# Matmuls of 512 columns issued as two of 256, one half of a PSUM bank after the other

## The reference, cut to what matters

```
nf, df = scan forward of (exp(k)*v, exp(k));  nb, db = the same backward
base = sigmoid(r) * ((nf + nb - ekv + euk*v) / max(df + db - ek + euk, 1e-8))
h = einsum('bsd,fd->bsf', base * (0.8 + 0.2*tf), W1)     # 1024 -> 4096
a = gelu(clip(round(h / 0.1)) * 0.1)
x + einsum('bsf,df->bsd', a, W2)                         # 4096 -> 1024
```

## Time and profile before

| | |
|---|---|
| time, median of 2 runs | 1900.47 us (1900.39 to 1900.55) |
| span of the profiled execution, first to last instruction | 1898.6 us |
| what lies around it, against the median | 1.9 us |
| TensorE busy | 1788.5 us (94%) |
| weight loads busy | 805.5 us (42%) |
| VectorE busy | 1342.6 us (71%) |
| ScalarE busy | 735.2 us (39%) |

### The profile page before, as it was taken

How to read it: one execution, slowest core, us unless ns; L and a number is a source line. 1 busy time by engine, 2 the same in 40 slices (tenths; PEclk the granted TensorE clock), 3 DMA queues, 4 the chain that set the end, 5 groups by cost and what they waited for, 6 DMA issues and landing times.

```text
span 1898.6 us, 24557 instructions
## 1 busy us (share of the span) xinstructions
PE 1788.5 (94%) x8194; PEld 805.5 (42%) x8194; DVE 1342.6 (71%) x1916; ACT 735.2 (39%) x1200; POOL 8.1 (0%) x20
## 2 busy tenths in 40 slices
PE   1358999999999999999999999999999999999998
PEld 0123444444444444444444444444444444444443
DVE  8986896698966796599986786588985777622111
ACT  4446611465116621366214641176313652034200
POOL 0000000000000000000000000000000000000000
PEclk9678999999999999999999999999999999999999
DMA  8585444434453344434443334534354334433133
GB/s 236 140 191 175 144 166 139 166 118 154 160 173 131 124 147 158 169 116 155 166 157 142 120 139 144 180 130 147 145 177 154 107 142 155 160 112 122 67 123 104
DMA packets 79576, 277.80 MB, mean 146 GB/s; under 512 B 9264, under 2 KB 9264, under 8 KB 62640
## 3 DMA queue, kind: packets, MB, share of 16 engines
q1 hardware_dynamic: 78768, 260.61, 39.3%
q0 software_dynamic: 768, 16.78, 4.3%
HBM read 277.36 MB, written 33.55 MB: 164 GB/s over the span
## 4 chain that ended last, share of the span: by engine, by line
PE 91%; DVE 5%; issue 2%; DMA 1%; ACT 0%; DVEq 0%; SPq 0%
PE h_ps L393 47%; PE h_ps L378 45%; DMA V<-in_fside_dram 1%; DVE DEN L636 1%; DVE EKP L633 0%; DVE NUM L660 0%; DVE NUM L681 0%; DVE DEN L664 0%; DVE EKV L630 0%; DVE DEN L670 0%; DVE V L667 0%; DVE EKVP L628 0%; DVE RCP L652 0%; DVE DEN L644 0%; DVE mix L588 0%
## 5 line engine op out<-in xcount | busy, mean ns | idle before, releaser
L393 PE MATMUL h_ps<-act,w_ring 128*128 128x512 f16 x4096 | 885.4, 379 | 0.0
L378 PE MATMUL h_ps<-mix,w_ring 128*128 128x512 f16 x3968 | 860.8, 380 | 8.6 <-ACT q L495 8.6
L393 PEld LDWEIGHTS h_ps<-act,w_ring 128*128 128x128 f16 x4096 | 400.8, 98 | 483.3
L378 PEld LDWEIGHTS h_ps<-mix,w_ring 128*128 128x128 f16 x3968 | 388.9, 98 | 479.2 <-ACT q L495 9.1
L805 DVE SCALAR_TENSOR_TENSOR act<-a,act 128x512 f32 (+1 forms) x256 | 164.9, 686 | 227.5 <-ACT act L508 227.3
L488 ACT ACTIVATE mix<-NUM 128x512 f32 (+1 forms) x64 | 40.1, 626 | 670.5 <-DVE NUM L783 623.9
L495 ACT ACTIVATE q<-h_ps 128x512 int16<-128x512 f32 x256 | 148.1, 591 | 333.2 <-PE h_ps L378 331.8
L812 DVE SCALAR_TENSOR_TENSOR xy<-h_ps,xy 128x512 f32<-128x512 f32 x64 | 43.9, 687 | 222.6 <-PE h_ps L393 222.6
L780 DVE RECIPROCAL DEN<-DEN 128x512 f32<-128x512 f32 x56 | 187.4, 3347 | 0.0
L502 ACT ACTIVATE a<-q 128x512 f32<-128x512 int16 x256 | 146.7, 622 | 0.6
L508 ACT ACTIVATE act<-a 128x512 f32 (+1 forms) x256 | 145.4, 617 | 0.0
(11 more groups left out here) (91 smaller groups left out, 903.7 us busy)
## 6 DMA issues: line engine op xcount, KB each, us to landing
w_ring<-w_half SPq DMA_DIRECT2D x128, 1024.0 KB, 4.9
chk_full<-in_w_dram SPq DMA_DIRECT2D x64, 512.0 KB, 5.7
V<-in_fside_dram SPq DMA_DIRECT2D x64, 256.0 KB, 4.3
R<-in_x_dram SPq DMA_DIRECT2D x64, 256.0 KB, 4.1
w_half<-in_w_dram POOLq DMA_DIRECT2D x16, 1024.0 KB, 11.4
xy<-in_x_dram SPq DMA_DIRECT2D x64, 256.0 KB, 2.7
chk_half<-w_half SPq DMA_DIRECT2D x64, 256.0 KB, 5.9
out_dram<-xy SPq DMA_DIRECT2D x64, 256.0 KB, 5.2
```

Source lines behind the costliest of these rows:

```text
L378: mm = pe.matmul(h_ps[k][j][:, :], weights[:, k, j, c, :], rhs, start=(c == 0 and p == 0), stop=(c == CT - 1 and p == len(parts(c)) - 1))
L393: mm = pe.matmul(y_ps[k][:, :], weights[:, k, f, :], rhs, start=(f == 0 and p == 0), stop=(f == FT - 1 and p == len(parts(f)) - 1))
```

## The change

`hidden` and `output` get a list of halves of the columns. For each tile, all matmuls of columns 0 to 255 are issued first, then all of columns 256 to 511, with the same weights again. The waits stand where they stood, ahead of a tile; in `output` those for `s_alo` are all in the first half. `start` (which empties the bank) is set on the first matmul of the first half alone. `first_hidden` isn't changed, and the general path asks for `WHOLE`, the old form.

```diff
+            HALF = [slice(0, T // 2), slice(T // 2, T)]
+            WHOLE = [slice(0, T)]
...
-            def hidden(n, i, weights, parts, loaded):
+            def hidden(n, i, weights, parts, loaded, halves=HALF):
...
-                        for c in range(CT):
-                            for p, rhs in enumerate(parts(c)):
-                                mm = pe.matmul(h_ps[k][j][:, :], weights[:, k, j, c, :], rhs,
-                                               start=(c == 0 and p == 0),
-                                               stop=(c == CT - 1 and p == len(parts(c)) - 1))
+                        for half in halves:
+                            for c in range(CT):
+                                for p, rhs in enumerate(parts(c)):
+                                    mm = pe.matmul(h_ps[k][j][:, half], weights[:, k, j, c, :], rhs[:, half],
+                                                   start=(half is halves[0] and c == 0 and p == 0),
+                                                   stop=(c == CT - 1 and p == len(parts(c)) - 1),
+                                                   skip_group_check=True)
                         mm.then_inc(s_h, 1)
...
-            def output(n, i, weights, parts, loaded, s_act, start):
+            def output(n, i, weights, parts, loaded, s_act, start, halves=HALF):
...
-                    for f in range(FT):
-                        if k == 0:
-                            pe.wait_ge(s_act[f % FPS], start + STEPS * n + f // FPS + 1)
-                        for p, rhs in enumerate(parts(f)):
-                            mm = pe.matmul(y_ps[k][:, :], weights[:, k, f, :], rhs,
-                                           start=(f == 0 and p == 0),
-                                           stop=(f == FT - 1 and p == len(parts(f)) - 1))
+                    for half in halves:
+                        for f in range(FT):
+                            if k == 0 and half is halves[0]:
+                                pe.wait_ge(s_act[f % FPS], start + STEPS * n + f // FPS + 1)
+                            for p, rhs in enumerate(parts(f)):
+                                mm = pe.matmul(y_ps[k][:, half], weights[:, k, f, :], rhs[:, half],
+                                               start=(half is halves[0] and f == 0 and p == 0),
+                                               stop=(f == FT - 1 and p == len(parts(f)) - 1),
+                                               skip_group_check=True)
                     mm.then_inc(s_y, 1)
```

More of the change, by code:

```diff
@@ L418, in general_block @@
                     hidden(n, i, w1_gen, lambda c: [mix_gen[:, slot, c, :]],
-                           lambda k: pe.wait_ge(s_wgen[k], 16 * (2 * ITER * m + i + 1)))
+                           lambda k: pe.wait_ge(s_wgen[k], 16 * (2 * ITER * m + i + 1)), WHOLE)
                 with pe.Fori(0, ITER) as i:
                     output(n, i, w2_gen, lambda f: [act_gen[:, f, :]],
-                           lambda k: pe.wait_ge(s_wgen[k], 16 * (2 * ITER * m + ITER + i + 1)), s_gelu, 0)
+                           lambda k: pe.wait_ge(s_wgen[k], 16 * (2 * ITER * m + ITER + i + 1)), s_gelu, 0, WHOLE)
             pe.wait_ge(s_flag, 1)
```

## The result

1934.88 us median (1934.33 to 1935.43, 2 runs) against 1900.47: a ratio of 1.018, 95% interval 1.015 to 1.021. The change costs 34 us. The forecast was 1925 us in a range of 1912 to 1950, so the sign and the range held, and the middle was 10 us low; the narrower range that the prediction adds up from its small terms, 1916 to 1934, was missed by 1 us. The interval holds 1.02, so whether the loss is more than the 2% that the prediction takes for a clear change isn't decided. The span of the profiled execution is 1931.1 us against 1898.6, 32.5 us more; the medians differ by 34.4. What lies outside the span is 3.2 and 3.0 us in the two runs of the change; in the other 37 runs of the kernel before it is 2.4 to 3.3, so the 1.9 beside the profile of before was unusually small.

The account below looks back on a forecast made before the run. The prediction took TensorE's unbroken chain of matmuls as the bound. Span 1898.6 + 20.1 (pace) + 4.0 (wait in block 0) = 1922.7 us; with 1.9 between span and median, 1924.6, stated as 1925, range 1912 to 1950.

Parts of the forecast that it names:

- small terms: Half clock after the wait in block 0, 0 to +3 us, and code fetches at outer jumps, 0 to +5 us.
- Term 1: In both products, 8018 matmuls each become two, paying a fixed 2.5 ns twice: 218.4 in place of 215.8 ns, +20.1 us.
- one that goes with columns: Rival, 5%: the 2.5 ns of each matmul go with its column count, so the pace costs nothing extra: 1904.5 us.
- Term 2: In block 0's `output`, TensorE wants activation tile 30 before DVE has written it, and waits: +4.0 us.
- 2.7 us of margin: In block 1's `output`, DVE's last tiles are done 3.9 us after the start, needed at 6.6: no wait.
- Term 3: After TensorE's 3.5 us stop in block 0, the clock might fall to half: taken as 0, range 0 to +3 us.
- Term 4: At two outer jumps, twice as many instructions might force code fetches: 0 to +5 us, taken as 0.
- The rival of the load: Every matmul of both products: the weight load comes into the open; with 16 ns settling, +77 us, 2002 us; 18%.
- 9 ns of margin: In both products, the 98 ns weight load still fits into a half matmul's 106.7 ns; the margin was 115 ns before.
- The faster rival: Half matmuls overlap down to a weight load's 98 ns, 180 us less than forecast: 1745 us; 2%.

Follow-up runs that it names:

- The kernel with the pace alone: The whole change plus TensorE's outer loop written out and, in the second product, both halves of an activation tile issued one behind the other: 1919.68 us, ratio 1.0098.
- its own control: The kernel before with only TensorE's outer loop written out: 1899.64 us against 1900.95 for the kernel before, ratio 0.9994.
- first and second experiment: The change in one product alone, against the kernel before: first product (`hidden`) 1910.53 us, ratio 1.0054; second product (`output`) 1917.48 us, ratio 1.0091.
- the kernel with the tiles side by side: The whole change, but in the second product both halves of an activation tile are issued one behind the other: 1925.02 us, ratio 1.0132 against the kernel before.
- The kernel before with a large body: The kernel before, matmuls still of 512 columns, with two turns written out in each inner body except the first of block 0: 1901.70 us, ratio 1.0004.
- four quarters: The change with both products in four parts of 128 columns in place of two of 256: one run, 1983.16 us.
- the three written-out kernels: TensorE's outer loop written out in the change (1926.72 us), in the kernel before (1899.64), and in the change with each tile's halves adjacent in the second product (1919.68).

## Why the prediction was right, and where it was short

**Term 1, the pace: right.** 111.79 / 1024 = 109.17 ns, the predicted 109.2, and 19.2 us for fifteen products. The choice between a fixed part and one that goes with columns is settled by three widths and a mixed pair: 55.84 - 53.33 = 2.51 ns at 128, 109.17 - 106.67 = 2.50 at 256, 215.84 - 213.33 = 2.51 at 512, and the pair of 320 and 192 costs the same 218.3 ns as two of 256. The kernel with the pace alone is 20.0 us above its own control.

**Term 2, the wait in block 0: right.** 3.63 us, as said, at tile 30, released by DVE L812. The 0.4 for tile 31 can't be read apart: the clock was at half by then, and the two matmuls of tile 30 took up much of it. It is in the second product alone (first and second experiment), and goes when a tile is wanted later (1925.0 us, no such wait). In block 1 and later no such wait shows, as was argued from the 2.7 us of margin.

**Term 3, the clock: taken at 0, was 2.9.** I argued from one wait of 8.6 us, where the clock fell 4.3 us after TensorE stopped, that a stop of 3.5 us would be too short. It wasn't: the clock was at half when TensorE restarted at 243.33, 3.6 us after, and at the second jump after a stop of 2.5 us. Behind the first jump (2.70 us) and behind both of the kernel with the tiles side by side (2.23 and 2.49) it wasn't. The length of the stop alone doesn't decide it: in the kernel with k = 0 kept at 512 the clock fell behind one of 2.19 us and not behind one of 2.24. Nor is the price fixed: with the loop written out, the same wait in block 0 (3.7 us) was followed by half clock from about 243 to 249 us and cost 2.9, the 3 us that I had named and set aside. One row doesn't bound when the clock falls; the spread is to be taken, here 0 to 2.9 us for each stop of some 2 to 4 us. That its two falls came to 2.9 us, inside the 0 to 3 I gave for one, is luck.

**Term 4, the code: taken at 0, was 5.6.** This is the step that failed. The bound (5 us for both jumps) was near, but not the value: I let matmuls already issued cover the fetch, without asking how long they last. A jump with a fetch takes 3.6 to 3.8 us in the change, and the issued matmuls last 1.8 of it. The kernel before with a large body shows the cover at 216 ns each, with 0.4 and 0.5 us left over. The control shows that the loop itself costs nothing. (The upper end of 1934 was also added wrongly: 1924.6 + 3 + 5 is 1932.6.) The Trainium skill's 2048 instructions (Runtime: NRT & Kernel Launch, Instruction fetch mechanics) gave the right answer for the change, 2,101, by my count above it; but 1,845 and 1,717 stopped too, and 1,589 didn't, so less than the 2048 can be used for a loop. The two lines of 256 that the same section gives (for a buffer of 32 KiB; TensorE's is 128) are refuted for TensorE again, in inner bodies of 512 instructions that never stop: 447 us between 350 and 797 without an idle moment.

**The rival of the load: wrong, and it needn't have had 18%.** I called 9 ns of margin thin. With four quarters a matmul comes every 55.8 ns, 42 ns less than a load lasts, and the pace is still its columns and 2.5 ns. The faster rival is refuted with it: 1024 matmuls in 111.79 us is the columns plus 2.5 ns.

Terms 3 and 4 are 8.5 us of the 10 by which the middle was low. The rest is that the medians differ by 1.9 us more than the spans. I added the 1.9 us around one span of the kernel before, where its other runs have 2.4 to 3.3 and the change has 3.0 and 3.2; what sets this part, and why it is 1.7 to 1.9 us in the three written-out kernels and in the one with two turns, no run here shows.

## What to carry to other kernels

In a kernel that TensorE bounds, a matmul of half the columns costs its columns and a fixed 2.5 ns (at full clock), which is 1% at 512 against 256 columns; weight loads beside it were free even where they outlast it (98 ns beside 55.8). Look instead at what the larger number of instructions does: whether the body of the outer loop is still kept, how long the issued matmuls last while code is fetched, and whether a sum that runs through its inputs in half the time overtakes those who write them. The stop at the jump and the wait for a late input could both be had back here by order alone: the loop written out, and the pieces of one input side by side.

## What the runs showed of the hardware that I had not expected

- A pair of weight load and matmul every 55.8 ns with loads of 98 ns each: loads overlap each other (16384 in 917 us of busy time).
- Changing the width of the stationary operand between 128 and 64 columns and back costs about 220 ns (one run), and a load of 64 columns lasts 110 ns.
- TensorE keeps an outer body of 1,589 instructions and fetches one of 1,717 again in each round: 18 packets of the instruction queue in 970 us, 21 at 1,845 and 2,101, and at 1,589 none once the loop jumps back.
- A jump back to code that has to be fetched takes 3.3 to 3.8 us, against 0.21 us, in bodies of 1,717 to 2,125 instructions; some 15 to 17 matmuls are issued ahead of it, and what they last is taken off the stop.
- A larger body doesn't stop more: two stops at a jump, of 2.2 and 1.9 us, 19 matmuls apart, at 1,845 instructions, and one of 2.7 us at 2,101. That it depends on where in the code the jump lands is a guess.
- The clock falls to half behind some stops of 2.2 to 3.7 us and not behind others of 2.2 to 2.7.
